# Squares added on VectorE, norm sums within gate tile 1, and the up product taken ahead of the reciprocal, in the MLP of a one-core attention and feed-forward kernel

## The reference, cut to what matters

```python
x1 = x + attn_out
h2 = _rms_norm(x1, ln2_w)          # x1 * rsqrt(mean(x1*x1) + eps) * w
mlp = jax.nn.silu(h2 @ w_gate) * (h2 @ w_up) @ w_down
processed = x1 + mlp
```

## Time and profile before

| what | value |
|---|---|
| median of 3 runs | 1623.16 us (1619.23 to 1624.06) |
| the profiled execution's own time | 1626.66 us |
| its span, first to last instruction | 1624.7 us |
| busy: TensorE / VectorE / ScalarE / GpSimd | 97% / 74% / 44% / 43% |
| share of TensorE in the chain that ended last | 89% |
| TensorE's granted clock, mean over the span | 0.986 of full |

### The profile page before, as it was taken

The page is one execution under the profiler, slowest core; times in us unless marked ns, Lnnn a source line. Parts: engine busy times, 40 slices in busy tenths (PEclk is TensorE's granted clock), DMA queues, the critical chain, the costliest instruction groups (busy, mean ns, idle before and its releaser), DMA issues.

```text
span 1624.7 us, 42309 instructions
## 1 busy us (share of the span) xinstructions
PE 1570.1 (97%) x16782; PEld 1216.7 (75%) x16782; DVE 1203.7 (74%) x1884; ACT 709.0 (44%) x1460; POOL 704.6 (43%) x785
## 2 busy tenths in 40 slices
PE   7999999999999999999999999999997999999897
PEld 5776777777777777777777777777775887777797
DVE  5753788878788787887788887878877585543886
ACT  5763444443444434444444444344444215555331
POOL 6761344344443344443444434444335681113642
PEclk9999999999999999999999999999998998999999
DMA  6842111112111122111121111221127233110000
GB/s 189 248 132 64 53 57 54 47 47 76 60 48 52 47 66 70 47 53 47 52 73 58 53 47 47 74 62 47 53 71 247 69 121 139 39 40 27 1 1 23
DMA packets 66167, 113.71 MB, mean 70 GB/s; under 512 B 21392, under 2 KB 36080, under 8 KB 64576
## 3 DMA queue, kind: packets, MB, share of 16 engines
q1 hardware_dynamic: 65280, 110.20, 21.4%
q0 software_dynamic: 832, 2.75, 0.6%
HBM read 82.59 MB, written 30.34 MB: 70 GB/s over the span
## 4 chain that ended last, share of the span: by engine, by line
PE 89%; ACT 5%; DVE 3%; POOL 1%; issue 1%; DMA 0%; ACTq 0%; POOLq 0%; DVEq 0%; SPq 0%
PE ps L1430 22%; PE ps L1431 19%; PE ps L1432 19%; PE ps L1560 8%; PE ps L1535 7%; PE ps L1508 3%; PE ps L1482 3%; PE ps L1764 2%; PE ps L1747 2%; ACT prob L778 2%; PE ps L1538 2%; PE ps L1756 1%; ACT prob L776 1%; PE ps L1464 1%; PE ps L1515 1%
## 5 line engine op out<-in xcount | busy, mean ns | idle before, releaser
L497 POOL TENSOR_TENSOR ctx_lo<-ctx_raw,ctx_hi 128x472 fp32r<-128x472 f32 x64 | 115.3, 1825 | 310.7 <-ACT ctx_hi L719 310.7
L534 POOL TENSOR_TENSOR prob_img<-prob 128x448 f32<-128x448 f32 x128 | 160.6, 1255 | 188.6 <-ACT prob L778 188.6
L1090 DVE RECIPROCAL rec<-ps 128x224 f32<-128x224 f32 x128 | 199.0, 1554 | 5.4 <-PE ps L1560 1.6
L776 ACT ACTIVATE prob<-ps 119x448 f32<-119x448 f32 x128 | 69.7, 545 | 209.2 <-PE ps L1538 209.2
L1079 DVE TENSOR_REDUCE top<-ps 112x4 f32<-112x1028 f32 x128 | 156.2, 1220 | 0.0
L1535 PEld LDWEIGHTS ps<-q_all,k_all 32*128 32x128 f32 (+1 forms) x3072 | 121.1, 185 | 45.4 <-issue 31.6
L1535 PE MATMUL ps<-q_all,k_all 32*128 32x112 f32 (+1 forms) x3072 | 147.4, 299 | 6.2 <-ACT prob L778 6.2
L752 ACT ACTIVATE sq_junk<-proj 128x513 bf16<-128x513 f32 (+1 forms) x96 | 61.2, 638 | 172.6 <-DVE proj L1058 172.6
L1078 DVE TENSOR_REDUCE top<-ps 112x4 f32<-112x472 f32 x128 | 83.0, 648 | 66.2 <-PE ps L1508 66.2
L1084 DVE SCALAR_TENSOR_TENSOR prob_img<-prob,ones_last,prob_img 23x448 f32<-23x448 f32 x128 | 90.3, 706 | 38.5 <-POOL prob_img L534 35.5
L778 ACT ACTIVATE prob<-ps 128x896 f32<-128x896 f32 x128 | 117.0, 914 | 0.0
(11 more groups left out here) (332 smaller groups left out, 4427.4 us busy)
## 6 DMA issues: line engine op xcount, KB each, us to landing
ctx_raw<-in_ctx_dram SPq DMA_DIRECT2D x32, 748.0 KB, 4.2
xh_dram<-xh SPq DMA_DIRECT2D x32, 448.0 KB, 3.1
q_dram<-q_turned SPq DMA_DIRECT2D x28, 256.0 KB, 2.7
q_all<-q_dram SPq DMA_DIRECT2D x32, 224.0 KB, 3.0
xh<-in_x_dram SPq DMA_DIRECT2D x32, 224.0 KB, 2.8
out_dram<-out_sb SPq DMA_DIRECT2D x32, 224.0 KB, 2.3
xa<-in_x_dram SPq DMA_DIRECT2D x21, 256.0 KB, 3.4
ring<-in_wq_dram SPq DMA_DIRECT2D x1, 4096.0 KB, 14.0
```

The source lines that it names most:

```text
L497: nc.gpsimd.tensor_tensor(ctx_lo[:, :, cols], ctx_raw[:, :, cols], ctx_hi[:, :, cols].bitcast(F32), ALU.subtract).then_inc(ctx_lo_done, 1)
L534: nc.gpsimd.tensor_tensor(prob_img[:, g % 2], prob[:, g % 2, 1, :], prob[:, g % 2, 2, :], ALU.add).then_inc(img_summed, 1)
L1090: nc.vector.reciprocal(rec[:], bank[:, 2:4]).then_inc(norm_step, 1)
```

## The change

It has three parts.

1. VectorE adds the four chunks of squares into one (three additions of 128x448), and TensorE's sum over the partitions has 4 matmuls where it had 16. It stands after the first chunk of tile 1's gate part, where it stood after tile 0.
2. VectorE takes up product times scaled gate directly after the scaled gate, and multiplies it by the reciprocal in place. The old product of scaled gate and reciprocal is gone. The semaphore `up_scaled` tells when neither PSUM bank is needed any more, and TensorE waits for it from tile 2 on.
3. ScalarE's two copies of the up product, and their buffer, are gone.

```diff
@@ ScalarE
-            def keep_up(j):
-                act.wait_ge(mlp_full, j + 1)
-                nc.scalar.activation(up_kept[:, j, :], ps[:, 5 + 2 * j, 0:S], ACT.Copy).then_inc(up_copied, 1)
-
             gate_up_rounded(2)
-            keep_up(0)
...
-                if j == 1:
-                    keep_up(1)
@@ VectorE
+            dve.wait_ge(mid_squared, 2)
+            nc.vector.tensor_tensor(mid_sq[:, 0, :], mid_sq[:, 0, :], mid_sq[:, 1, :], ALU.add).then_inc(squares_added, 1)
+            dve.wait_ge(mid_squared, KC)
+            nc.vector.tensor_tensor(mid_sq[:, 2, :], mid_sq[:, 2, :], mid_sq[:, 3, :], ALU.add).then_inc(squares_added, 1)
+            dve.wait_ge(squares_added, 2)
+            nc.vector.tensor_tensor(mid_sq[:, 0, :], mid_sq[:, 0, :], mid_sq[:, 2, :], ALU.add).then_inc(squares_added, 1)
             dve.wait_ge(sums_full, 1)
...
                 nc.vector.tensor_tensor(g_, gate_, rstd_row[:], ALU.mult).then_inc(gate_scaled, 1)
+                dve.wait_ge(gate_scaled, j + 1)
+                nc.vector.tensor_tensor(m_prod[:, j % 2, :], up, g_, ALU.mult).then_inc(up_scaled, 1)
                 if j:
                     hidden_rest(j - 1)
                 dve.wait_ge(silu_exp, j + 1)
                 nc.vector.tensor_scalar(e, e, 1.0, None, ALU.add).then_inc(silu_step, 1)
-                dve.wait_ge(silu_step, 3 * j + 1)
+                dve.wait_ge(silu_step, 2 * j + 1)
                 nc.vector.reciprocal(e, e).then_inc(silu_step, 1)
-                dve.wait_ge(silu_step, 3 * j + 2)
-                nc.vector.tensor_tensor(g_, g_, e, ALU.mult).then_inc(silu_step, 1)
-                dve.wait_ge(silu_step, 3 * j + 3)
-                if j < 2:
-                    dve.wait_ge(up_copied, j + 1)
-                    up = up_kept[:, j, :]
-                nc.vector.tensor_tensor(m_prod[:, j % 2, :], up, g_, ALU.mult).then_inc(hid_ready, 1)
+                dve.wait_ge(silu_step, 2 * j + 2)
+                dve.wait_ge(up_scaled, j + 1)
+                nc.vector.tensor_tensor(m_prod[:, j % 2, :], m_prod[:, j % 2, :], e, ALU.mult).then_inc(hid_ready, 1)
@@ TensorE
                     pe.wait_ge(gate_up_lo_done, j + 1)
-                    if 2 <= j < 4:
-                        pe.wait_ge(gate_scaled, j - 1)
-                        pe.wait_ge(up_copied, j - 1)
-                    elif j >= 4:
-                        pe.wait_ge(hid_ready, j - 1)
-                    gate_or_up(j, 0)
+                    if j >= 2:
+                        pe.wait_ge(up_scaled, j - 1)
                     if j == 1:
+                        gate_or_up(1, 0, range(0, 1))
+                        pe.wait_ge(squares_added, 3)
+                        for c in range(NC):
+                            made = nc.tensor.matmul(ps[0:L, 0, c:c + 1], mid_sq[:, 0, c * L:(c + 1) * L], ones_col[:], start=True, stop=True)
+                        made.then_inc(sums_full, 1)
+                        gate_or_up(1, 0, range(1, KC))
                         pe.wait_ge(rstd_ready, 3)
                         turn_row(1, rstd)
                         pe.wait_ge(root_ready, 3)
                         turn_row(2, sums)
+                    else:
+                        gate_or_up(j, 0)
                     gate_or_up(j, 1).then_inc(mlp_full, 1)
-                    if j == 0:
-                        pe.wait_ge(mid_squared, KC)
-                        for c in range(NC):
-                            for kc in range(KC):
-                                made = nc.tensor.matmul(ps[0:L, 0, c:c + 1], mid_sq[:, kc, c * L:(c + 1) * L], ones_col[:], start=kc == 0, stop=kc == KC - 1)
-                        made.then_inc(sums_full, 1)
```

More of the change, by code:

```diff
@@ L248, in build @@
         over_cos_k.close()
-        up_kept = over_cos_k.enter_context(nc.sbuf_tensor("up_kept", [P, 2, S], F32))
-        over_cos_k.close()
         cos_k = sb("cos_k", [P, S])
@@ L310, in build @@
         row_full, row_ready, mid_scaled = sem("row_full"), sem("row_ready"), sem("mid_scaled")
-        gate_scaled, up_copied = sem("gate_scaled"), sem("up_copied")
+        gate_scaled, up_scaled, squares_added = sem("gate_scaled"), sem("up_scaled"), sem("squares_added")
         mid_kept, processed_ready, turned_back = sem("mid_kept"), sem("processed_ready"), sem("turned_back")
@@ L1803, in down, with gate_or_up @@
                     last.then_inc(down_step, 1)
-            def gate_or_up(j, e):
+            def gate_or_up(j, e, chunks=range(KC)):
                 lo = (w_gate_lo, w_up_lo)[e]
-                for kc in range(KC):
+                for kc in chunks:
                     if j == 0 and e == 0:
```

## The result

| | before | after |
|---|---|---|
| median of runs | 1622.33 us (1619.23 to 1624.06, 6 runs) | 1612.66 us (1611.27 to 1614.95, 6 runs) |
| profiled execution, its span | 1626.66, 1624.7 us | 1612.68, 1610.7 us |

The ratio is 0.9935, with a 95% interval of 0.9923 to 0.9947: **faster by 10.5 us (8.6 to 12.5)**. The forecast was 1612.2 us. The two medians as they stand differ by 9.7 us, inside that interval. The two profiled executions differ by more, 14.0 us, since the one of before lay some 4 us above its median. So a term read from the two traces can't be set against the medians without a look at what that execution happened to carry.

What follows compares the result with a forecast made beforehand. TensorE was taken to bound the kernel, with VectorE's chain setting the pace up to tile 4. Terms 3.4 + 5.27 + 2.5 - 0.2 = 11.0 us off the 1623.16 us median gave 1612.2 us, range 1606.5 to 1618.5.

Steps and rivals of the forecast that it cites:

- wait ahead of the four sums, and the sums: TensorE within tile 1's gate part: 0.2 us waiting for VectorE's additions, then four sums in about 0.8 us.
- tile 3 earlier: TensorE's start of tile 3 at 1498.5 us, 3.4 us earlier, since VectorE's chain starts earlier and tile 0 is shorter.
- wait ahead of tile 4: TensorE ahead of tile 4: the 5.27 us standstill goes whole, since only up_scaled of tile 2 is needed.
- tile 4 earlier: TensorE's start of tile 4: 8.7 us earlier.
- low clock behind it (tile 5 earlier): The 10.12 us window behind tile 4's wait: 37 matmuls at full clock take 7.65 us, gaining 2.5; bounds 0 and 5.
- the end: Last down part: chain 0.1 us shorter, but GpSimd may hold the addition; a loss of 0.2 us taken.
- The sums and the row: Norm's sums and row in tile 1: sums gain 1.4 us, clock stays full, up part starts 3.2 us earlier.
- Tile 0: VectorE's tile 0: 6.69 us becomes 6.0, plus 0.2 for an addition held by GpSimd (net 0 to 0.45).
- Rival 3: Ahead of tiles 3, 4 and 5: the 5.27 us wait only moves, leaving a 3.4 us gain, 1619.8 us; chance 0.05.
- Tiles 5 to 15: TensorE sets 7.44 us a tile, VectorE has 6.5 to 6.7 to do: no gain.
- Rivals 1 and 4: First: GpSimd holds the addition in every tile, 1613.3 us, chance 0.22; fourth: VectorE bounds tiles 5 to 15, chance 0.03.
- Rival 4: Tiles 5 to 15: VectorE becomes the bound, passing TensorE at holds of 1.4 us a tile; 1639 us, chance 0.03.

Runs made afterwards that it cites:

- The fillers in the kernel before: Kernel before with 22 unread matmuls of 448 columns added ahead of tile 4, so TensorE works during the wait: 1620.26 us, ratio 0.9977.
- the sums alone: Kernel before with only the three VectorE additions and 4 sums within tile 1's gate part; old product order and release kept: 1620.27 us, ratio 0.9970.
- fillers in attention: Changed kernel with nine unread matmuls ahead of attention's first scores: 1614.23 us; in the second run also tile 2's weights split right behind tile 1's: 1611.74 us.

## Why the prediction was right

| step | forecast | traces |
|---|---|---|
| wait ahead of the four sums, and the sums | 0.2 + 0.8 us | 0.18 + 0.81 |
| tile 3 earlier | 3.4 | 3.28 |
| wait ahead of tile 4 | 5.27 gone whole | gone |
| tile 4 earlier | 8.7 | 8.68 |
| low clock behind it (tile 5 earlier) | 2.5 (11.2) | 2.7 (11.39) |
| the end | -0.2 | 0 |
| the whole | 11.0 | 10.5 (8.6 to 12.5) by the runs |

**The sums and the row.** The two dependent additions took 0.63 and 0.62 us, the near bound. The clock stayed full, the second row's transposes waited 0.3 us as computed, and the up part of tile 1 started where it should. The sixteen sums in the new place show that the additions, not the place, carry this step. The 3.4 us hold 1.6 us of low clock behind the sums, which fell in three of five profiles; in an execution where it does not fall, this step is worth less.

**Tile 0.** It took 6.27 us against the forecast 6.0 + 0.2. The addition lost 0.54, and the last product, now later, found less to wait for. The *bound* of this step was wrong: I let a held addition lose at most 0.8 us, what line 1409 loses, and the experiments showed 3.9 and 4.3 us. The range still held the median, and the two profiles near that median show a hold of 0.54 us alone; how many executions have the long one is not known.

**The wait ahead of tile 4.** It went whole, and with the old release it came back as 3.39 us. The forecast put the tile of VectorE at 6.69 us at most; tiles 1 and 2 took 6.16 and 6.15, a gain that the sum does not have and did not need. Rival 3, by which the wait only moves, is refuted: from tile 2 to the last down part no wait over 0.3 us is left.

**The low clock.** 2.5 us was one execution's spell, and the two profiles give 2.7. The fillers in the kernel before gave 3.7 (2.1 to 5.2), which may hold some of the spacing below.

**Tiles 5 to 15 and the end.** I gave nothing here. Two things happened that the sum lacks. The matmuls followed one another at 0.2027 us in place of 0.2067, worth 1.7 us from tile 5 to the last down part; whether the change has a part in that is open (below). And at the end `m_lo` of tile 15 was done 7.04 us after its scaling (1590.43 to 1597.47), so the loss of 0.2 did not come.

**Rivals 1 and 4.** The addition started about 0.1 us ahead of GpSimd's instruction in the other tiles and kept its 0.39 us, as the forecast had it. Pushed over that edge, all but the last took 1.48 or more, and VectorE's tile was still shorter than TensorE's. Rival 4's point of decision, 1.4 us of holds a tile, was not reached even there.

**Against the profiles.** Their difference of 14.0 us is 0.9 ahead of the MLP, 11.4 up to tile 5, and 1.7 of matmul spacing. The forecast took the differences off the median as if each execution of before carried all terms. The mechanism is shown; that the sum hits the median to within 0.5 us is partly luck. It counts a low clock behind the sums that some executions don't have, and it leaves out the shorter VectorE tile, which the release hides, and the spacing of the matmuls.

## What to carry to other kernels

Where a buffer is given back by the last of several steps that read it, look whether that read can come first: moving one product ahead of a 2.95 us reciprocal took away a wait of 5 us, and the low clock behind it, without making any engine faster. With the new order but the old release 3.39 us of the wait were left. Count what the clock does behind a wait as a cost of its own, and price it over several executions. And keep GpSimd empty where a VectorE instruction on the critical path reads SBUF alone; here a tile in mid-stream could stand such a hold, the first one could not.

## What the runs showed of the hardware

**A held VectorE instruction can be passed over.** The addition (one SBUF input) and GpSimd's subtraction of SBUF operands kept each other out: 0.93, 1.48, 4.27 and 4.71 us in place of 0.39 us, and GpSimd's own 1.30 us grew to 1.43 behind an addition that came first, and to 1.66 behind `m_lo` (both operands in SBUF) that came first. The Trainium skill (SBUF — State Buffer, Who interferes with whom) has the exclusion, for a whole instruction. By that rule the trace agrees with 0.93 and 1.48. The 4.27 and 4.71 us go beyond it: there VectorE waited through the rest of one GpSimd instruction and three more back to back. What decides whether it gets in between two of them stays open.

**The clock behind a wait is not fixed by its length alone.** It fell behind waits of TensorE of 5.1 to 5.3, of 3.53 and 3.55, of 2.37 and (ahead of attention's scores, in eleven profiles of twelve) of 2.17 us. It stayed full behind one of 3.39, and in the twelfth profile behind 2.17.

**The spacing of matmuls has two values.** At full clock, matmuls of 448 columns followed one another through tiles 5 to 15 at 0.2027 or at 0.2067 us. The changed kernel has the first in its two profiles, and the second with four sums behind tile 0 and in both runs with fillers in attention, so the release does not set it. The kernel before and that with the sums alone, the three profiles with a wait of over 5 us ahead of tile 4 and a low clock behind it, all have the second; the kernel before with that wait filled has the first. So it may be chance, or the wait may have a part in it; three profiles don't settle that. The value changed only at a gap in TensorE's stream and then held until the next. It is worth 1.7 us, its cause was not tried and is open, and it is one more reason why two single profiles differ by more than their kernels do.
